# Three-stride attention and the second expert sorting in one unrolled stage, on one NeuronCore

## The chip, the cores and the metric

The kernel runs on one core of one Trainium2 chip. What counts is the device time of one execution in microseconds; the median of the kernel before is 2400.16 us over three runs (2399.35 to 2404.34).

## The reference

An input of 256 images of 128 channels and 7 x 7 places goes through four layers: a windowed attention with a bias table, a group norm with a single-head attention, a plain attention with a mixture of experts (8 experts of hidden width 192, the best 2 for each token), and the layer that the change is in. Cut to that layer:

```python
t = t + _L3_attn_ref(_ln_t(t), Wq, bq, Wk, bk, Wv, bv)   # t: 256 images, 49 tokens, 128 channels
t = t + _L3_ffn_ref(_ln_t(t), Wr, br, W1, b1, W2, b2)

# _L3_attn_ref: x + positional encoding, then 8 heads of 16
for sc in (1, 2, 4):                       # every key, every 2nd, every 4th
    scores = einsum('bhqd,bhkd->bhqk', qh, kh[::sc]) * scale
    outs.append(einsum('bhqk,bhkd->bhqd', softmax(scores), vh[::sc]))
out = mean(outs)
# _L3_ffn_ref: the router's top 2 of 8 experts for each token, hidden 512
combine = zeros(N, E).at[arange(N), top2].add(sel_w / sum(sel_w))
out = einsum('ne,end->nd', combine, gelu(x @ W1 + b1) @ W2 + b2)
```

## The kernel before

The activations stay in SBUF as X, 128 channels by 12544 tokens in fp32, through the whole kernel. The program is a row of stages, each a block of its own in which every engine has its own instruction stream and the engines meet through semaphores only; a barrier stands between two stages. In order: `heads_phase` (windowed attention), `single_phase` (group norm and its attention), `token_dispatch_phase` (plain attention and the first sorting, `d2`), `blocks_phase` (experts, `moe2`), `combine_phase`, `scales_phase` (three-stride attention), `dispatch_phase` (the second sorting, `d3`), `blocks_phase` (`moe3`), `final_phase`.

`scales_phase` (L1156) works on 32 groups of 8 images, 392 tokens each. It runs in steps, one for each group, and each step has four quarters p = 0 to 3, one for each pair of images. `pair(s, p, ahead)` names the pair that is `ahead` pairs further than pair 4s + p. The stages of the work on a pair or a group lie at different distances, so that the engines work on different groups at once: PE computes scores 3 pairs ahead (L1307), DVE takes the maximum of each key class and subtracts it 2 pairs ahead (L1403, L1407), ACT takes the exponential 1 pair ahead (L1628), DVE sums it (L1416), POOL multiplies the probabilities 8 pairs behind (L1528), PE turns them 9 pairs behind (L1332), ACT copies them out (L1646), and PE multiplies them with the values 10 pairs behind (L1350). The weights of the three strides are worked out once for a group from the class maxima and sums, by turns on DVE (`highest`, `totals`, `factors`), POOL (`lower`, `parts`, `shares`) and ACT (`lowered`). The norm of a group (DVE, L1392) runs 2 groups ahead. The bias and scale of the output are on ACT (L1655), the residual on POOL (L1543). Four quarters of a step are written out by hand in a fixed order for each engine; `over_steps` (L720) unrolls the first and last steps and loops over four steps at a time between them.

The class `Dispatch` (L1724) sorts tokens by expert. For a chunk of 4 tiles of 128 tokens: PE turns the tiles (`turn`, L1828) and computes the router's logits (`logits`, L1839); DVE takes the statistics (`stats`, L1946, L1953); ACT makes the reciprocal root (`rstd`) and DVE the negated mean (`negmean`, L1961); ACT writes the normed rows (`norm`, L1898); DVE scales the logits (`scale`, L1970), takes the two highest (`choose`) and counts; PE adds up ranks (`positions`); ACT and DVE add the gate columns (`gate`, `names`, `weigh`), DVE the row numbers (`place`); and POOL sends each row twice, to the region of either expert, by an indirect DMA of 128 rows of 132 floats (`scatter`, L2093). There are 98 tiles, so 196 scatters. Three buffers of rows go round, and a buffer's scatters must have landed before it is written again. Beside this, ACT and DVE split the weights of the 8 experts in a high and a low part (L1876, L1937), which SP loads and stores.

`dispatch_phase` (L2389) is nothing but these steps, with four PSUM banks for the turned tiles. `token_dispatch_phase` runs the same class beside an attention, unrolled, with POOL free for the scatters alone.

## Time and profile before

| what | value |
|---|---|
| median of three runs | 2400.16 us |
| profiled execution | 2404.97 us |
| its span | 2403.2 us |
| PE busy | 1784.2 us, 74% of the span |
| DVE busy | 1668.8 us, 69% |
| POOL busy | 1428.9 us, 59% |
| ACT busy | 1370.0 us, 57% |
| mean granted clock of TensorE | 0.861 of 2.4 GHz |

The profiled execution took 1.8 us more than its span, which runs from the first to the last instruction, and 4.8 us more than the median. The busy shares are means over stages with different limits, so a stage's own stretch has to be read. Times in the rows are microseconds from the span's start; PEld is the load of PE's weights, and PEclk is the granted clock as a share of 2.4 GHz.

### The profile page before, as it was taken

The page shows a single profiled execution, that of the slowest core. Times are in us where ns is not written, and L with a number is a line of the kernel's source. Part 1 is how long each engine was busy: PE and PEld are TensorE (multiplying, and loading weights), DVE is VectorE, ACT ScalarE, POOL GpSimd, SP SyncE. Part 2 cuts the span into 40 slices and gives each one's busy share as a digit, 9 for nine tenths or more (in the row PEclk, how much of TensorE's full clock was granted, in tenths as well). Part 3 has the DMA queues.
Part 4 walks back from the last instruction along what each step waited for, and adds up shares of the span by engine and source line. Part 5 has one row for each costly group of instructions (what it writes and reads, how often), then busy time and mean ns, then how long its engine had stood idle before and what let it go on. Part 6 is the DMA issues. An engine that isn't in the chain of part 4 may idle for free. (4 is left out here: it accounts for less than half of the span.)

```text
span 2403.2 us, 53239 instructions
## 1 busy us (share of the span) xinstructions
PE 1784.2 (74%) x16241; PEld 1241.7 (52%) x16241; DVE 1668.8 (69%) x4819; ACT 1370.0 (57%) x2989; POOL 1428.9 (59%) x1509
## 2 busy tenths in 40 slices
PE   7999997997777527777647888886333159999983
PEld 3555554774555415555433555554322147777763
DVE  5888886884878626656546898884654447888864
ACT  5777774564666325555406898883322147777760
POOL 4565562110577737767763667764777737767765
PEclk9999998998988569998958999995555579999995
DMA  6000000001311146665450000002611347777747
GB/s 118 9 0 0 0 1 1 1 0 41 104 55 55 55 124 182 179 174 161 140 218 1 2 0 0 0 1 57 211 64 54 90 159 232 232 233 225 231 150 321
DMA packets 169793, 233.09 MB, mean 97 GB/s; under 512 B 60032, under 2 KB 131957, under 8 KB 162190
## 3 DMA queue, kind: packets, MB, share of 16 engines
q1 hardware_dynamic: 142446, 172.32, 24.2%
q0 software_dynamic: 26880, 52.27, 6.4%
q10 hardware_dynamic: 288, 6.42, 0.6%
q8 instruction: 75, 1.23, 0.2%
q14 instruction: 104, 0.85, 0.1%
HBM read 155.37 MB, written 79.23 MB: 98 GB/s over the span
## 5 line engine op out<-in xcount | busy, mean ns | idle before, releaser
L2689 POOL DMA_INDIRECT expert_out<-moe_yr,moe_to x448 | 495.8, 1107 | 260.1 <-DVE moe_yr L2668 137.5
L2093 POOL DMA_INDIRECT expert_rows<-d_row,d_pos x392 | 380.6, 971 | 198.9 <-issue 177.5
L2604 ACT ACTIVATE moe_ah<-moe_hps,moe_w 128x512 f32<-128x512 f32 (+1 forms) x336 | 230.1, 685 | 209.4 <-PE moe_hps L2554 207.1
L2645 DVE TENSOR_TENSOR moe_hl<-moe_ah,moe_hh 128x512 fp32r<-128x512 f32 (+1 forms) x336 | 235.5, 701 | 101.1 <-ACT moe_hh L2609 95.2
L1898 ACT ACTIVATE d_row<-d_xt,d_nm,d_drs 128x128 f32<-128x128 f32 x196 | 73.8, 456 | 181.6 <-DMA expert_rows<-d_row,d_pos 179.0
L550 POOL TENSOR_TENSOR window_pr<-window_pr,window_rc 113x392 f32<-113x392 f32 x128 | 108.9, 851 | 106.5 <-DVE window_rc L494 106.4
L2552 PE MATMUL moe_hps<-moe_xh,moe_w 128*128 128x512 f32 (+1 forms) x336 | 139.0, 414 | 37.6 <-DMA moe_w<-moe_split 28.6
L1839 PE MATMUL d_small<-d_wgc,X 128*128 128x8 f32 x392 | 74.7, 318 | 113.3 <-DVE d_at L2035 113.3
L2540 PE MATMUL moe_xps<-ident,moe_xb 128*128 128x128 f32 x448 | 73.4, 289 | 113.1 <-DMA moe_xb<-expert_rows 113.0
L2564 PE MATMUL moe_yps<-moe_hh,moe_w 128*128 128x512 f32 (+1 forms) x336 | 144.5, 430 | 0.9 <-DVE moe_hl L2645 0.9
L538 POOL TENSOR_TENSOR window_sc<-window_sc,window_mx 113x392 f32<-113x392 f32 x128 | 107.8, 842 | 50.4 <-DVE window_mx L468 49.5
L2554 PE MATMUL moe_hps<-moe_xh,moe_w 128*128 128x512 f32 (+1 forms) x336 | 134.8, 401 | 0.0
L2553 PE MATMUL moe_hps<-moe_xl,moe_w 128*128 128x512 f32 (+1 forms) x336 | 134.8, 401 | 0.0
L2565 PE MATMUL moe_yps<-moe_hl,moe_w 128*128 128x512 f32 (+1 forms) x336 | 134.0, 399 | 0.0
L2566 PE MATMUL moe_yps<-moe_hh,moe_w 128*128 128x512 f32 (+1 forms) x336 | 133.9, 398 | 0.0
L1839 PEld LDWEIGHTS d_small<-d_wgc,X 128*128 128x128 f32 x392 | 73.6, 280 | 116.2 <-DVE d_at L2035 116.2
L2540 PEld LDWEIGHTS moe_xps<-ident,moe_xb 128*128 128x128 f32 x448 | 54.2, 146 | 144.3 <-DMA moe_xb<-expert_rows 135.6
L1332 PE MATMUL scales_ptps<-ident,scales_pr 113*128 113x113 f32 x512 | 90.7, 287 | 48.7 <-DVE scales_sc L1407 33.8
L2634 DVE TENSOR_TENSOR moe_xl<-moe_xps,moe_xh 128x512 fp32r<-128x512 f32 x112 | 76.4, 682 | 66.7 <-ACT moe_xh L2597 66.7
L1528 POOL TENSOR_TENSOR scales_pr<-scales_pr,scales_fac 113x416 f32<-113x416 f32 x128 | 114.7, 898 | 12.5 <-DVE scales_fac L1447 12.5
L657 ACT ACTIVATE window_pt<-window_ptps 128x452 f32<-128x452 f32 x128 | 69.8, 545 | 90.0 <-PE window_ptps L334 89.9
L2609 ACT ACTIVATE moe_hh<-moe_ah 128x512 fp32r<-128x512 f32 (+1 forms) x168 | 106.2, 632 | 5.3
(270 smaller groups left out, 5185.2 us busy)
## 6 DMA issues: line engine op xcount, KB each, us to landing
moe_w<-moe_split SPq DMA_DIRECT2D x56, 1026.5 KB, 5.2
moe_xb<-expert_rows SPq DMA_DIRECT2D x112, 264.0 KB, 3.0
moe_w<-moe_split SPq DMA_DIRECT2D x56, 449.5 KB, 3.5
c_yy<-expert_out SPq DMA_DIRECT2D x28, 448.0 KB, 6.5
final_yy<-expert_out SPq DMA_DIRECT2D x28, 448.0 KB, 7.0
expert_out<-moe_yr,moe_to POOLq DMA_INDIRECT x448
X<-in_x SPq DMA_DIRECT2D x32, 196.0 KB
expert_rows<-d_row,d_pos POOLq DMA_INDIRECT x392, 2.3
```

What stands on the lines that cost most here:

```text
L1839: last = pe.matmul(self.small[:, i * EXPERTS:(i + 1) * EXPERTS], self.sh.X[:, (t0 + i) * C:(t0 + i + 1) * C], self.wgc[:, :], start=True, ...
L2093: pool.indirect_dma_start(out=self.rows_dram, out_offset=bass.IndirectOffsetOnAxis(ap=self.pos[j][:, i, k:k + 1], axis=0), in_=self.row[j] ...
L2540: last = pe.transpose(xps[:, t * C:(t + 1) * C], xb[b % NX][:, t, 0:C], ident[:, :])
L2552: pe.matmul(out, ww[:, W1H + k * P:W1H + (k + 1) * P], xh[j][:, :], start=True, stop=False)
L2553: pe.matmul(out, ww[:, W1H + k * P:W1H + (k + 1) * P], xl[j][:, :], start=False, stop=False)
L2554: pe.matmul(out, ww[:, W1L + k * P:W1L + (k + 1) * P], xh[j][:, :], start=False, stop=True).then_inc(h_mm, 1)
L2564: pe.matmul(out, ww[0:P, W2H + k * C:W2H + (k + 1) * C], high, start=(k == 0), stop=False)
L2565: pe.matmul(out, ww[0:P, W2H + k * C:W2H + (k + 1) * C], low, start=False, stop=False)
L2566: pe.matmul(out, ww[0:P, W2L + k * C:W2L + (k + 1) * C], high, start=False, stop=(k == K - 1)).then_inc(y_mm, 1)
L2604: act.activation(ah[n % NH][0:P, :], hps[n % 3][0:P, :], func, bias=bias(b, k)[0:P]).then_inc(h_done, 1)
L2645: dve.tensor_tensor(hl[n % NH][0:P, :], ah[n % NH][0:P, :], hh[n % NH][0:P, :].bitcast(F32), ALU.subtract).then_inc(hl_done, 1)
L2689: pool.indirect_dma_start(out=y_dram, out_offset=bass.IndirectOffsetOnAxis(ap=to[j][:, t:t + 1], axis=0), in_=yr[j][:, t, :], in_offset=No ...
```

## The change

`scales_phase` and `dispatch_phase` go, and `scales_dispatch_phase` does the work of both. The steps are fully unrolled, from s = -3 to 37. Chunks of the second sorting hold 3 tiles (384 tokens) and not 4, 32 of them and one of 2. In step s, PE, DVE and ACT sort chunk s - 4, and POOL sends the scatters of chunk s - 5, six in a row, behind its last quarter. One PSUM bank holds three turned tiles and, in its last quarter, logits and ranks; to free banks, the centred tile and the queries share one, and the variance uses the bank of the values' products. The factor 1/3 goes into the value weights at the start, so the residual, its bias included, is one DVE instruction from PSUM; ACT's output copy and POOL's addition go. Both halves of the values' copy are on ACT. `shares` and `lowered` come one place earlier. The first sorting keeps its chunks.

```diff
-CHUNKS = chunk_tiles()
+CHUNKS_D2 = chunks_of([4] * 24 + [2])
+CHUNKS_D3 = chunks_of([3] * 32 + [2])
...
+        def steps(body):
+            for s in range(-LEAD, NG + LATE + 3):
+                body(Step(s, s))
...
+            def turn_rows(c):
+                pe.wait_ge(res_done, min(c + 1, NG))
+                if c >= 1:
+                    pe.wait_ge(d.normed, c)
+                d.logits(pe, c, c)
+                d.turn(pe, c)
...
+            def ranks(c):
+                pe.wait_ge(d.normed, c + 1)
+                d.positions(pe, c, c + 1)
...
             def body(s):                                  # PE
                 for p in range(PAIRS):
                     turn(*pair(s, p, -9), pair(s, p, 3))
+                    if p == 0:
+                        turn_rows(chunk(s, -4))
                     scores(*pair(s, p, 3))
+                    if p == 3:
+                        ranks(chunk(s, -4))
...
+            def residual(at):
+                dve.wait_ge(pv_mm, (at.g + 1) * PAIRS)
+                dve.scalar_tensor_tensor(out=X[:, cols(at.g)], in0=ops_[:, 0:T], scalar=b_use[:, 2:3], in1=X[:, cols(at.g)],
+                                         op0=ALU.add, op1=ALU.add).then_inc(res_done, 1)
             def body(s):                                  # DVE
+                c = chunk(s, -4)
                 for p in range(PAIRS):
+                    if p == 2:
+                        residual(s.ahead(-3))
                     shift(*pair(s, p, 2))
+                    if p == 1 and c is not None:
+                        d.negmean(dve, c)
+                        d.scale(dve, c)
                     total(*pair(s, p, 0))
                     if p == 0:
                         norm(s.ahead(2))
+                        if c is not None:
+                            d.stats(dve, c)
+                        if due(s.g - 1) and s.g % 3 == 1 and s.g // 3 <= EXPERTS:
+                            d.split_low(dve, s.g // 3 - 1)
                     if p == 1:
                         highest(s)
+                            d.choose(dve, c)
+                    if p == 2:
+                            d.count_up(dve, c)
                     if p == 3:
                         factors(s.ahead(-1))
+                            d.weigh(dve, c)
+                            d.place(dve, c)
...
             def body(s):                                  # POOL
                     if p == 2:
                         lower(s)
-                    if p == 3:
-                        shares(s.ahead(-1))
-                        residual(s.ahead(-3))
+                    if p == 2:
+                        shares(s.ahead(-1))
+                    c = chunk(s, -5)
+                    if c is not None and p == PAIRS - 1:
+                        d.scatter(pool, c)
...
+                        act.wait_ge(d.scaled, c + 1)      # ACT, p == 1
+                        d.norm(act, c)
...
-            scales_phase(nc, sh, scales)
-        dispatch_phase(nc, sh, "d3", MOE3, w3, rows_dram)
+            scales_dispatch_phase(nc, sh, scales, "d3", MOE3, w3, rows_dram)
```

On POOL, one step of the attention before, the last that is unrolled ahead of the loop, from its first quarter on (`scales_pr` with the quarter's number are the probabilities):

```order
L1528 TENSOR_TENSOR scales_pr_0<-scales_pr_0,scales_fac 113x8x52
L1537 TENSOR_TENSOR scales_xn<-scales_xn,pos 128x8x49
L1528 TENSOR_TENSOR scales_pr_1<-scales_pr_1,scales_fac 113x8x52
L1509 TENSOR_TENSOR scales_part<-scales_ef,scales_sm 113x384
L1528 TENSOR_TENSOR scales_pr_2<-scales_pr_2,scales_fac 113x8x52
L1497 TENSOR_TENSOR scales_low<-scales_mx,scales_top 113x128
L1498 TENSOR_TENSOR scales_low<-scales_mx,scales_top 113x64
L1528 TENSOR_TENSOR scales_pr_3<-scales_pr_3,scales_fac 113x8x52
L1519 TENSOR_TENSOR scales_wf<-scales_ef,scales_rc 113x384
L1543 TENSOR_TENSOR X<-X,scales_ot 128x392
```

The same step on POOL in the changed kernel:

```order
L2014 TENSOR_TENSOR scales_pr_0<-scales_pr_0,scales_fac 113x8x52
L2023 TENSOR_TENSOR scales_xn<-scales_xn,pos 128x8x49
L2014 TENSOR_TENSOR scales_pr_1<-scales_pr_1,scales_fac 113x8x52
L1995 TENSOR_TENSOR scales_part<-scales_ef,scales_sm 113x384
L2014 TENSOR_TENSOR scales_pr_2<-scales_pr_2,scales_fac 113x8x52
L1983 TENSOR_TENSOR scales_low<-scales_mx,scales_top 113x128
L1984 TENSOR_TENSOR scales_low<-scales_mx,scales_top 113x64
L2005 TENSOR_TENSOR scales_wf<-scales_ef,scales_rc 113x384
L2014 TENSOR_TENSOR scales_pr_3<-scales_pr_3,scales_fac 113x8x52
L1563 DMA expert_rows<-d_row,d_pos 107008x132
L1563 DMA expert_rows<-d_row,d_pos 107008x132 x5
```

The residual on X is gone, the shares stand a place earlier, and six scatters stand ahead of the next step's first probabilities.

On DVE in the changed kernel, the third quarter of a step and the start of the fourth (`scales_ops` are the products with the values, `scales_tot` and `scales_rc` the totals and their reciprocals, `d_` are tiles of the sorting):

```order
L1924 SCALAR_TENSOR_TENSOR X<-scales_ops,scales_b_use,X 128x392
L1874 TENSOR_REDUCE scales_mx<-scales_sps 113x32
L1878 TENSOR_TENSOR scales_sc<-scales_sps,scales_mx 113x416
L1905 TENSOR_REDUCE scales_tot<-scales_part 113x96
L1909 RECIPROCAL scales_rc<-scales_tot 113x96
L1887 TENSOR_REDUCE scales_sm<-scales_pr_2 113x32
L1466 CAST d_idf<-d_idx 128x6
L1470 TENSOR_TENSOR d_pick<-iota,d_idf 128x48
L1476 TENSOR_TENSOR d_seen<-d_pick 128x24
L1479 TENSOR_REDUCE d_more<-d_seen 128x8
L1483 TENSOR_TENSOR d_count<-d_count,d_more 128x8
L1874 TENSOR_REDUCE scales_mx<-scales_sps 113x32
```

Before, this quarter held the shift, the sum, the totals and the copy of the values; now the residual stands ahead of the shift, the totals ahead of the sum, and the sorting's counts behind it.

## Rows read from the trace of the kernel before

**Rows 1.** Busy time by stretch: us, PE, PEld, DVE, ACT, POOL (instructions), PEclk, DMA share, GB/s

```profile
1300.00:1640.00 340.00, 293.34 (x4490) 176.37 (x4486) 299.73 (x565) 294.69 (x581) 233.02 (x295) 0.96 0.00 1
1683.00:1918.00 235.00, 70.20 (x403) 59.45 (x403) 121.67 (x815) 55.87 (x211) 179.49 (x183) 0.50 0.32 104
```

**Rows 2.** Timeline at the borders: start, us, engine, line, instruction [idle before <- releaser]

```profile
1253.00 1.99 POOL L1478 MEMSET scales_pr<- 113x96 f32 x16 [4.07 <-POOLq L101]
1325.23 0.57 DVE L1392 TENSOR_TENSOR scales_xn<-scales_cen,scales_rs 128x392 f32<-128x392 f32 x1 [0.66 <-ACT scales_rs L1599]
1928.58 0.95 POOL L2093 DMA_INDIRECT expert_rows<-d_row,d_pos  x1 [0.30 <-issue]
1939.54 1.28 ACT L2589 ACT_TABLE_LOAD   x1 [33.03 <-PEq L101]
```

**Rows 3.** Groups by line, sorting stage, 1683 to 1918: busy us, mean ns | idle before

```profile
L2093 POOL DMA_INDIRECT expert_rows<-d_row,d_pos x183 | 179.9, 983 | 55.8 <-issue 55.5 <-DVE d_row L2027 0.3
L1961 DVE SCALAR_TENSOR_TENSOR d_nm<-d_mv,d_drs 128x4 f32<-128x4 f32 (+1 forms) x23 | 3.7, 162 | 51.5 <-ACT d_drs L1888 51.5
```

**Rows 4.** Timeline of DVE, one step of the attention, 1449.5 to 1462

```profile
1449.95 0.57 DVE L1392 TENSOR_TENSOR scales_xn<-scales_cen,scales_rs 128x392 f32<-128x392 f32 x1 [1.26 <-ACT scales_rs L1599]
...
1452.96 0.59 DVE L1403 TENSOR_REDUCE scales_mx<-scales_sps 113x32 f32<-113x416 f32 x1 [0.20 <-PE scales_sps L1307]
...
1456.05 0.69 DVE L1456 COPY scales_vbd<-scales_vps 52x512 f32<-52x512 f32 x1
...
1461.39 0.57 DVE L1392 TENSOR_TENSOR scales_xn<-scales_cen,scales_rs 128x392 f32<-128x392 f32 x1 [0.67 <-ACT scales_rs L1599]
```

**Rows 5.** Groups by line of POOL, attention, 1300 to 1640

```profile
L1528 POOL TENSOR_TENSOR scales_pr<-scales_pr,scales_fac 113x416 f32<-113x416 f32 x120 | 107.8, 899 | 12.5 <-DVE scales_fac L1447 12.5
L1509 POOL TENSOR_TENSOR scales_part<-scales_ef,scales_sm 113x384 f32<-113x384 f32 x30 | 30.1, 1004 | 38.9 <-ACT scales_ef L1637 38.9
L1537 POOL TENSOR_TENSOR scales_xn<-scales_xn,pos 128x392 f32<-128x392 f32 x28 | 28.9, 1033 | 56.8 <-DVE scales_xn L1392 56.8
L1519 POOL TENSOR_TENSOR scales_wf<-scales_ef,scales_rc 113x384 f32<-113x384 f32 x29 | 25.2, 868 | 0.0
L1497 POOL TENSOR_TENSOR scales_low<-scales_mx,scales_top 113x128 f32<-113x128 f32 x30 | 12.4, 414 | 0.0
L1498 POOL TENSOR_TENSOR scales_low<-scales_mx,scales_top 113x64 f32<-113x64 f32 x30 | 9.2, 306 | 0.0
```

**Rows 6.** The scatters of the first sorting stage, 600 to 960

```profile
L2093 POOL DMA_INDIRECT expert_rows<-d_row,d_pos x196: 954/958/1142, 618.6 to 865.3; - x196
```

**Rows 7.** One line of the convolution stage, its bias and residual: ns min/median/max

```profile
L1045 DVE SCALAR_TENSOR_TENSOR X<-conv_ops,conv_b_use,X x32: 615/620/627, 419.8 to 558.8; 128x392 f32 x24, 128x392 f32<-128x392 f32 x8
```

**Rows 8.** Timeline of DVE, one chunk of the sorting stage

```profile
1702.32 0.19 DVE L1970 TENSOR_TENSOR d_lg<-d_small,d_drs 128x32 f32<-128x32 f32 x1 [1.44 <-PE d_small L1839]
...
1706.37 1.19 DVE L1937 TENSOR_TENSOR d_wl<-d_raw,d_wh 128x1024 f32<-128x1024 f32 x1
1707.48 0.16 DVE L1961 SCALAR_TENSOR_TENSOR d_nm<-d_mv,d_drs 128x4 f32<-128x4 f32 x1
...
1708.63 0.17 DVE L2045 CAST d_pos<-d_spot 128x8 uint32<-128x8 f32 x1
```

**Rows 9.** Timeline, the start of the second sorting stage

```profile
1682.63 1.19 DVE L1937 TENSOR_TENSOR d_wl<-d_raw,d_wh 128x1024 f32<-128x1024 f32 x1
1682.74 1.91 POOL L2093 DMA_INDIRECT expert_rows<-d_row,d_pos  x1 [0.30 <-issue]
```

**Rows 10.** Busy time by stretch, the first sorting stage

```profile
650.00:700.00 50.00, 38.07 (x331) 28.94 (x330) 42.23 (x232) 33.98 (x115) 37.80 (x41) 0.93 0.17 55
750.00:800.00 50.00, 37.39 (x286) 30.05 (x286) 36.90 (x209) 28.13 (x94) 37.81 (x41) 0.78 0.17 55
```

**Rows 11.** Timeline of PE, attention, high clock and low

```profile
1452.33 0.56 PE L1307 MATMUL scales_sps<-scales_kbd,scales_qt 64*64 64x196 f32 x8
1623.02 0.93 PE L1307 MATMUL scales_sps<-scales_kbd,scales_qt 64*64 64x196 f32 x8
```

More of the change, by code:

```diff
@@ L1153, in _, with __init__, tiles_of @@
             over_steps(act, body, LEAD)
-def scales_phase(nc, sh, weights):
+class Experts:
+    def __init__(self, hidden):
+        self.hidden = hidden
+        self.part = C if hidden % C == 0 else 96
+        self.chunks = hidden // self.part
+        self.half = hidden + self.chunks * C
+        self.bias_at = 2 * self.half
+        self.width = 2 * self.half + self.chunks + 1
+MOE2, MOE3 = Experts(192), Experts(512)
+def tiles_of(c):
+    return range(c * CHUNK, min(TILES, (c + 1) * CHUNK))
@@ L1162, in scales_phase, with sorting_steps, scales_dispatch_phase @@
+def sorting_steps(quads, groups_done):
+    turns, step = [], 0
+    for c, t0, nt, o in quads:
+        while groups_done(step) * T < (t0 + nt) * C:
+            step += 1
+        turns.append(step)
+        step += 1
+    return turns
+def scales_dispatch_phase(nc, sh, weights, kind, e, wsplit, rows_dram):
     SCALES = 3
@@ L1219, in scales_phase, with chunk, _ @@
         block = ctx.enter_context(nc.Block())
+        def steps(body):
+            for s in range(-LEAD, NG + LATE + 3):
+                body(Step(s, s))
+        def chunk(s, ahead):
+            c = s.g + ahead
+            return c if 0 <= c < len(d.chunks) else None
+        @block.sync
+        def _(sp):
+            d.weights(sp)
+            d.pads(sp)
         def pair(s, p, ahead):
@@ L1368, in body @@
                         var(s.ahead(3))
-            over_steps(pe, body, LEAD, LATE)
+            steps(body)
+            d.totals(pe)
         @block.vector
@@ L1662, in v_out @@
                     act.wait_ge(pv_mm, (at.g - 1) * PAIRS)
-                dst, src = v_places(at, 0)
-                act.activation(dst, src, ACT.Copy).then_inc(v_left, 1)
+                for r in range(2):
+                    dst, src = v_places(at, r)
+                    last = act.activation(dst, src, ACT.Copy)
+                last.then_inc(v_done, 1)
             def body(s):
+                c = chunk(s, -4)
                 for p in range(PAIRS):
@@ L2101, in sorting_steps @@
-def sorting_steps(groups_done):
-    turns, step = [], 0
-    for c, t0, nt, o in QUADS:
-        while groups_done(step) * T < (t0 + nt) * C:
-            step += 1
-        turns.append(step)
-        step += 1
-    return turns
+                        if c is not None:
+                            d.names(act, c)
+                        if due(s.g) and s.g % 3 == 0 and s.g // 3 <= EXPERTS:
+                            d.split_high(act, s.g // 3 - 1)
+            steps(body)
 def token_dispatch_phase(nc, sh, kind, e, wsplit, rows_dram):
@@ L2160, in chunks @@
         def chunks(step):
-            return [c for c, q in enumerate(LAST_QUAD) if turns[q] == step]
+            return [c for c, q in enumerate(d.last_quad) if turns[q] == step]
         @block.sync
@@ L2232, in _ @@
                 for c in chunks(s - 2):
[L2233 removed]
+                    d.positions(pe, c, len([k for k in range(len(d.chunks)) if turns[d.last_quad[k]] <= s - 1]))
                 if group(s):
@@ L2244, in _ @@
                 for c in chunks(s):
-                    d.logits(pe, c, len([k for k in range(len(CHUNKS)) if turns[LAST_QUAD[k]] <= s - 2]))
+                    d.logits(pe, c, len([k for k in range(len(d.chunks)) if turns[d.last_quad[k]] <= s - 2]))
             d.totals(pe)
@@ L2462, in _ @@
+            for c in range(len(d.chunks)):
                 d.scatter(pool, c)
```

853 lines of the change are left out of this document (388 added, 465 removed).

## The prediction

> **What bounds the kernel now.** I first read the busy time by stretch. In the attention of the three strides, 340 us of its steady part, DVE is busy 299.7 us, ACT 294.7, PE 293.3 and POOL only 233.0; in the sorting stage behind it POOL is busy 179.5 of 235 us, and PE 70.2 and DVE 121.7 [rows 1]. The reader is to see two neighbouring stages with opposite limits. The borders of the stages come from the timeline: the attention starts at 1253.00, the last scatter at 1928.58, and the first work of the expert stage behind it at 1939.54 [rows 2]. The two stages together take 1939.54 - 1253.00 = 686.5 us.
>
> The groups by line say what sets the second stage: 183 scatters take 983 ns each and POOL is idle 0.30 us before each for "issue", with hardly another releaser [rows 3]. So POOL sends one scatter in (179.9 + 55.8) / 183 = 1.29 us, and 196 of them make the stage; everything else there waits. In the attention one group of images takes 11.44 us: two norms of the centred tile start at 1449.95 and 1461.39, and between them DVE stands still only 0.20 us, before a maximum, and 0.67 us, before the second norm [rows 4]. DVE sets this stage, with ACT close behind.
>
> **What the change does, by step.** The scatters go to POOL in the attention's own steps, six in each, and the sorting work of 3 tiles goes to DVE, ACT and PE there. The stage of its own (with its starting loads, and its first chunk before a scatter can go) is gone. I work out the length of a step X and then count steps.
>
> *POOL.* Four probability products at 899 ns, 1.00 for the parts, 1.03 for the position, 0.87 for the shares, 0.41 + 0.31 for the two differences; the residual leaves POOL [rows 5]: 3.60 + 3.62 = 7.22 us. Six scatters at the undisturbed spacing, 0.958 + 0.30 us as in the first sorting stage [rows 6], are 7.55. POOL needs 14.8 us.
>
> *DVE.* From 11.44 the copy of the values goes (0.69, now on ACT) [rows 4]; the residual comes, with the bias in one instruction that reads PSUM, as in the convolution stage: 0.62 [rows 7]. The sorting of 4 tiles took 4.05 us from the scaled logits to the end of the statistics, and 1.23 from the negated mean to the next scatter's release (1707.48 to 1708.71, 0.08 behind the start of the last row) [rows 8]: 5.3. With 3 tiles, one of four maxima, index searches, statistics and aggregations goes, about 0.6 in all: 4.7. Eight subtractions that split the weights, 1.19 each [rows 8], spread over 27 steps are 0.33. Sum: 11.44 - 0.69 + 0.62 + 4.7 + 0.33 = 16.4 us. The 0.87 us of idle time in 11.44 stays in it. I keep it because the longer step gives more slack to the old waits, but DVE gets two new ones: for PE's transposes of the three tiles, which now stand between a turn and the next scores, and for ACT's reciprocal root before the negated mean. Bounds: no waiting at all puts X at 16.4 - 0.87 = 15.5; the 51.5 / 23 = 2.2 us that DVE stands a chunk before the negated mean in the sorting stage [rows 3], on top of the 0.87, put it at 18.6. I take the present 0.87 alone, since it is from the stage with the longer work to wait behind.
>
> *ACT and PE.* ACT is busy 294.7 / 30 = 9.8 us a step; it loses the scaled output (0.57), gains the other half of the values and about 2 us of sorting: 12. PE is busy 293.3 / 30 = 9.8 and gains three transposes, six small products and the ranks, about 1.4 at the high clock: 11.2. Both stay under 16.4.
>
> *The burst.* The new wait is on POOL's queue: behind the six scatters stand the next step's probabilities, for which PE's turn and, behind it, the scores in program order wait. After DVE's reciprocal POOL has 0.87 + 0.90 + 7.55 + 0.90 = 10.2 us until the first pair of the next step is ready; turn and scores add 1.1, so the scores stand at 11.3. DVE begins the shift that reads them 16.4 - 1.3 (totals) - 1.1 (the shift) = 14.0 us after its reciprocal. The burst is hidden, by 2.7 us. If that cover went, each us of it would be added to X.
>
> *Shared interface.* One scatter took 1.91 us where DVE ran the weights' subtraction, which reads two SBUF tiles, beside it; undisturbed ones take 0.958 [rows 6, 9]. Eight of them cost POOL 8 x 0.95 = 7.6 us, 0.3 per step, and POOL has 1.6 to spare: nothing on the path. The Trainium skill (GPSIMD Engine Reference, Key points) says that POOL shares its SBUF interfaces with DVE and contends with DVE instructions that have two SBUF inputs. By that rule the small products of the sorting would stretch scatters too. The first sorting stage speaks against it: all 196 scatters beside the same small DVE work and an attention lay between 954 and 1142 ns [rows 6]. The sum stays at zero here.
>
> *The count.* The steps up to the norm of group 6, at 1325.23, have no sorting in them [rows 2]; the start is about 2 us later, since DVE and PE now wait for the sorting's constants. From there 27 steps of X carry both. After the norm's place in step 31 POOL still needs 18.4 us to the end of that step's burst (9.0 on DVE to the reciprocal, then 0.87 + 0.90 + 7.55), then 13.0 (3.60 + 1.00 + 0.87 + 7.55) and 11.2 (3.60 + 7.55) for the two steps that still have probabilities, three times 7.6 and a last 5.1: 52.1; the sorting's own chain, by the spacing of its steps some 8 us a chunk, runs beside it. Landing and barrier are 10.0, as from 1929.53 to 1939.54 now [rows 2]. The expert stage then starts at 1325.2 + 2 + 27 x 16.4 + 18.4 + 52.1 + 10.0 = 1407.7 + 27 x 16.4 = 1850.5, which is 89.0 us earlier than 1939.5. What is behind it does not change. The profiled execution took 2404.97 us, so 2316.0; it lies 4.8 above the median of the three runs, 2400.16, and against that I predict **2311 us**.
>
> **Rivals.**
> 1. *DVE without its waits, POOL at its floor.* X = 15.1 from POOL's 14.8 and the 0.3 of stretched scatters, and 0.1 for the handover, 15.2; the stage ends at 1818, 2279 us. For it: the first sorting stage runs exactly at its scatters. Against: DVE alone has 15.5 without a wait.
> 2. *PE's clock is low for part of the time.* At the busy share of the first sorting stage (38.1 and 37.4 of 50 us) the granted clock was 0.93 and 0.78, so between 1.2 and 2.4 GHz by turns [rows 10]. PE would be busy only 11.2 of 16.4 us here. Scores for a pair take 0.56 us at the high clock and 0.93 at the low one [rows 11], 1.66 times as long: PE then needs 11.2 x 1.66 = 18.6 us and, with its present 1.6 of waiting, X = 20.2. With three tenths of the time low, as those two rows have it on average, X = 1 / (0.7 / 16.4 + 0.3 / 20.2) = 17.4: 1877.5, 2338 us. Against: the slack of 5 us takes short dips.
> 3. *PE's clock stays low throughout: slower than before.* X = 20.2 gives 1407.7 + 545.4 = 1953.1, 13.6 us later than now, 2414 us. It decides from X = 19.7 on, where the stage ends as before. For it: the second sorting stage had 0.50 throughout [rows 1]. Against: at the low clock PE would be busy 18.6 of 20.2 us, and at 293 of 340 the attention's clock was 0.96 [rows 1].
>  The Trainium skill (TensorE: Matmul & The Clock Gate, HAM oscillation) says that gaps in PE's work make the gate fall back to half rate. By that rule a step with a long wait behind the burst would fall back each time, which is this rival; without such a wait rival 2 at most.
> 4. *The burst is not hidden.* If the 7.55 us came on top of the present step, X = 19.0 and 2381 us. It needs turn, scores and shift to be waiting at once, which the 2.7 us above speak against.
>
> **How the numbers follow.** Forecast 0.45, rival 1 0.17, rival 2 0.22, rival 4 0.06, rival 3 and other ways beyond X = 19.7 0.08, the strip around no change 0.02. About 0.2% (4.8 us) is what a measurement of this kernel can tell from no change. The range runs from below rival 1, where the tail is also a little shorter, 2270, to X = 18.6, 1909.9, 2370. Faster 0.90, same 0.02, slower 0.08.
>
> **What would show it.** The spacing of the attention's norms in steady state near 16.4; POOL busy about 13.3 of it with its "issue" gaps; DVE busy about 14.5; scatters near 0.96 us, none above 1.2 but those beside the weights' subtraction; the wait of PE's turn for POOL's probabilities small; DVE's waits for PE before the statistics and for ACT before the negated mean, together near 1 us a step; the granted clock at 0.85 or more; some 50 us of scatters behind the last group. I am wrong if the spacing is beyond 18.6, if PE's turns wait for POOL by more than 1 us each step, or if the clock stays at 0.5.

## The result and the profile after

The changed kernel takes 2389.26 us (median of five runs, 2388.34 to 2391.54) beside 2402.08 us of the kernel before on the same chip: a ratio of 0.995, 95% interval 0.9935 to 0.9964. It is faster by 12.8 us, which is clear of the noise but only 0.5%, where 89 us were forecast, and it lies outside the range. The profiled span went from 2403.2 to 2389.8 us.

The page's busy times of the changed kernel, and its two sorting and attention lines:

```profile
PE 1850.0 (77%) x16257; PEld 1271.8 (53%) x16257; DVE 1759.3 (74%) x4940; ACT 1380.3 (58%) x3028; POOL 1400.3 (59%) x1477
...
L1563 POOL DMA_INDIRECT expert_rows<-d_row,d_pos x392 | 377.7, 964 | 180.0 <-issue 175.4
...
L2014 POOL TENSOR_TENSOR scales_pr<-scales_pr,scales_fac 113x416 f32<-113x416 f32 x128 | 115.6, 905 | 6.6 <-DVE scales_fac L1918 6.0
```

DVE is busy 90.5 us longer than before, for work that hardly changed. The merged stage begins at 1253.86 and the expert stage's first instruction comes at 1926.85, so it takes 673.0 us; the two stages before took 686.5. The steady part, busy time by stretch, and the norms of groups 6, 8 and 31 on DVE's timeline (`scales_xn`), the last two 23 steps apart:

```profile
1360.00:1800.00 440.00, 331.98 (x3785) 203.86 (x3783) 391.03 (x1124) 285.95 (x648) 293.70 (x342) 0.77 0.14 46
```

```profile
1326.88 0.57 DVE L1863 TENSOR_TENSOR scales_xn<-scales_cen,scales_rs 128x392 f32<-128x392 f32 x1 [1.40 <-ACT scales_rs L2082]
...
1361.07 0.57 DVE L1863 TENSOR_TENSOR scales_xn<-scales_cen,scales_rs 128x392 f32<-128x392 f32 x1 [1.06 <-ACT scales_rs L2082]
...
1805.49 0.57 DVE L1863 TENSOR_TENSOR scales_xn<-scales_cen,scales_rs 128x392 f32<-128x392 f32 x1 [0.99 <-ACT scales_rs L2082]
```

A step is (1805.49 - 1361.07) / 23 = 19.3 us and not 16.4, and DVE is busy 391 of 440 us in it (columns as in [rows 1]), 89%. Where its time went stands in the groups by line of the same stretch, DVE alone; the last row is one that is not held up:

```profile
L1426 DVE SCALAR_TENSOR_TENSOR d_nm<-d_mv,d_drs 128x3 f32<-128x3 f32 x23 | 45.3, 1969 | 3.9 <-ACT d_drs L1353 3.5
L1402 DVE TENSOR_TENSOR d_wl<-d_raw,d_wh 128x1024 f32<-128x1024 f32 x7 | 25.6, 3663 | 0.1
L1476 DVE TENSOR_TENSOR d_seen<-d_pick 128x24 bf16<-128x24 f32 x23 | 18.3, 794 | 0.8
L1470 DVE TENSOR_TENSOR d_pick<-iota,d_idf 128x48 f32<-128x48 f32 x23 | 10.8, 471 | 0.8
L1454 DVE TENSOR_TENSOR d_gap<-d_top 128x3 f32<-128x3 f32 x23 | 7.1, 308 | 0.8
L1897 DVE TENSOR_TENSOR scales_top<-scales_mx 113x32 f32<-113x32 f32 x23 | 4.6, 201 | 0.0
```

The first five of them as the kernel before has them in its sorting stage, with 4 tiles instead of 3:

```profile
L1937 DVE TENSOR_TENSOR d_wl<-d_raw,d_wh 128x1024 f32<-128x1024 f32 x6 | 7.3, 1209 | 7.3 <-ACT d_wh L1876 7.3
...
L2000 DVE TENSOR_TENSOR d_pick<-iota,d_idf 128x64 f32<-128x64 f32 (+1 forms) x22 | 4.9, 223 | 0.8
L2006 DVE TENSOR_TENSOR d_seen<-d_pick 128x32 bf16<-128x32 f32 (+1 forms) x22 | 4.7, 213 | 0.8
...
L1989 DVE TENSOR_TENSOR d_gap<-d_top 128x4 f32<-128x4 f32 (+1 forms) x22 | 3.6, 165 | 0.8
L1961 DVE SCALAR_TENSOR_TENSOR d_nm<-d_mv,d_drs 128x4 f32<-128x4 f32 (+1 forms) x22 | 3.6, 162 | 51.5 <-ACT d_drs L1888 51.5
```

A negated mean of 3 numbers a partition takes 1969 ns instead of 162. All five have two inputs in SBUF (two tensors, or for `d_seen` and `d_gap` two parts of one); so has the sixth, at a place where POOL stands still. Per step that is 1.81 + 0.58 + 0.25 + 0.14, and 7 x 2.45 / 23 = 0.75 for the splits: 3.5 us. What POOL does meanwhile is seen when the two timelines of one step are laid side by side, POOL's first:

```profile
1468.03 0.87 POOL L2005 TENSOR_TENSOR scales_wf<-scales_ef,scales_rc 113x384 f32<-113x384 f32 x1 [3.41 <-DVE scales_rc L1909]
1468.86 0.90 POOL L2014 TENSOR_TENSOR scales_pr<-scales_pr,scales_fac 113x416 f32<-113x416 f32 x1
1469.90 1.01 POOL L1563 DMA_INDIRECT expert_rows<-d_row,d_pos  x1 [0.15 <-issue]
...
1476.27 0.96 POOL L1563 DMA_INDIRECT expert_rows<-d_row,d_pos  x1 [0.30 <-issue]
1477.25 0.91 POOL L2014 TENSOR_TENSOR scales_pr<-scales_pr,scales_fac 113x416 f32<-113x416 f32 x1
1478.11 1.03 POOL L2023 TENSOR_TENSOR scales_xn<-scales_xn,pos 128x392 f32<-128x392 f32 x1
1479.09 0.90 POOL L2014 TENSOR_TENSOR scales_pr<-scales_pr,scales_fac 113x416 f32<-113x416 f32 x1
1479.95 0.99 POOL L1995 TENSOR_TENSOR scales_part<-scales_ef,scales_sm 113x384 f32<-113x384 f32 x1
1480.90 0.88 POOL L2014 TENSOR_TENSOR scales_pr<-scales_pr,scales_fac 113x416 f32<-113x416 f32 x1
...
1486.88 0.87 POOL L2005 TENSOR_TENSOR scales_wf<-scales_ef,scales_rc 113x384 f32<-113x384 f32 x1 [3.41 <-DVE scales_rc L1909]
```

```profile
1478.68 0.59 DVE L1878 TENSOR_TENSOR scales_sc<-scales_sps,scales_mx 113x416 f32<-113x416 f32 x1
1479.20 2.60 DVE L1426 SCALAR_TENSOR_TENSOR d_nm<-d_mv,d_drs 128x3 f32<-128x3 f32 x1
1481.73 0.17 DVE L1435 TENSOR_TENSOR d_lg<-scales_sorted,d_drs 128x24 f32<-128x24 f32 x1
...
1486.05 0.75 DVE L1909 RECIPROCAL scales_rc<-scales_tot 113x96 f32<-113x96 f32 x1
```

POOL's row of five elementwise products behind the six scatters ends at 1481.78. The negated mean, begun at 1479.20, ends at 1481.80. **A loop** goes through both engines: from DVE's reciprocal POOL waits for no other engine, through shares, product, burst and row, from 1468.03 to 1481.78, 13.75 us; only then does DVE get past the negated mean, and needs 5.1 us to the next reciprocal; POOL goes on at 1486.88. 13.75 + 5.10 = 18.85 us is this step. It is not the only one: of the 18 negated means between 1360 and 1700, 15 end within 0.05 us behind the row's last product, and the other three stand behind a split of 4.9 or 5.6 us that had waited for the row in their place. The waits say the same without naming it: POOL stands 3.41 us for the reciprocal in every one of the 23 steps, though in the step above DVE works without a gap meanwhile.

### The profile page after: what moved, and what is told of

The parts are those of the page before. It is cut to its first block and busy times, and to the rows that moved or that the text cites. A ratio compares the mean times of both kernels' runs of the same rounds, so it can differ in the third digit from the quotient of the medians.

```text
span 2389.8 us, 52820 instructions
## 1 busy us (share of the span) xinstructions
PE 1850.0 (77%) x16257; PEld 1271.8 (53%) x16257; DVE 1759.3 (74%) x4940; ACT 1380.3 (58%) x3028; POOL 1400.3 (59%) x1477
## 5 line engine op out<-in xcount | busy, mean ns | idle before, releaser
L1780 PE MATMUL scales_ptps<-ident,scales_pr 113*128 113x113 f32 x512 | 113.9, 332 | 135.4 <-DVE scales_sc L1878 122.5
L1780 PEld LDWEIGHTS scales_ptps<-ident,scales_pr 113*128 113x128 f32 x512 | 74.0, 173 | 189.1 <-DVE scales_sc L1878 113.8
L2129 ACT ACTIVATE scales_pt<-scales_ptps 128x452 f32<-128x452 f32 x128 | 69.7, 545 | 125.0 <-PE scales_ptps L1780 124.6
L2632 DVE CAST moe_hh<-moe_ah 128x512 fp32r<-128x512 f32 (+1 forms) x168 | 88.3, 525 | 27.1 <-ACT moe_ah L2593 27.1
```

Of the source, the lines that this page charges most:

```text
L1780: last = pe.transpose(ptps[:, hp * R:(hp + 1) * R], pr[at.r][p][:, 2 * hp:2 * hp + 2, :].rearrange("q h k -> q (h k)"), ident[0:R, 0:R])
```

## The experiments

X is the spacing of the norms of groups 8 to 31. The stage runs from POOL's first fill to the expert stage's table load; its start moves by some us between kernels, since the stages ahead of it do. PE's granted clock is that of 1400 to 1700. Every kernel ran beside the kernel before (medians 2399.6 to 2402.8). The expectations say VectorE for DVE, GpSimd for POOL, ScalarE for ACT and TensorE for PE.

| kernel | median us | ratio to before (95%) | stage us | X us | PE clock |
|---|---|---|---|---|---|
| changed kernel | 2389.3 | 0.995 (0.9935 to 0.9964) | 673.0 | 19.3 | 0.77 |
| negated mean later | 2381.4 | 0.991 (0.988 to 0.994) | 669.5 | 19.25 | 0.76 |
| negated mean, one input | 2377.5 | 0.990 (0.987 to 0.994) | 661.6 | 18.9 | 0.76 |
| all moved | 2367.9 | 0.987 (0.983 to 0.991) | 654.8 | 18.6 | 0.79 |
| three pairs of scatters | 2324.6 | 0.968 (0.9645 to 0.972) | 610.7 | 16.9 | 0.81 |
| two scatters early | 2336.1 | 0.973 (0.971 to 0.976) | 621.1 | 17.4 | 0.82 |
| unlocked | 2312.1 | 0.963 (0.960 to 0.967) | 588.1 | 16.1 | 0.86 |
| unlocked, three pairs | 2342.3 | 0.975 (0.972 to 0.979) | 614.7 | 17.1 | 0.80 |
| unlocked, one put back | 2363.8 | 0.985 (0.983 to 0.987) | 634.1 | 17.8 | 0.81 |
| unlocked, statistics later | 2457.9 | 1.023 (1.020 to 1.026) | 729.5 | 21.4 | 0.72 |
| unlocked, PE busier | 2317.6 | 0.9655 (0.964 to 0.967) | 587.2 | 15.9 | 0.94 |
| unlocked, two early | 2317.3 | 0.966 (0.964 to 0.968) | 589.8 | 16.2 | 0.84 |

### Is it the two inputs, and does the time go when they are moved?

My first theory (A) took the held-up instructions as a price per instruction. Three kernels remove that price in different ways.

```diff
-                    if p == 1 and c is not None:
-                        d.negmean(dve, c)
-                        d.scale(dve, c)
...
                         highest(s)
                         if c is not None:
+                            d.negmean(dve, c)
+                            d.scale(dve, c)
                             d.choose(dve, c)
```

> The negated mean (128x3, two SBUF inputs) and the scaled logits go behind the first and second maximum of the same quarter, to a place where GpSimd has come to the end of its row of products. In the changed kernel the negated mean took 1.94 us on average, 0.16 in the kernel before. Theory A (a VectorE instruction with two SBUF inputs can't start while GpSimd runs elementwise products one behind the other): it takes 0.2 to 0.5 us, the step goes from 19.3 to about 17.7 us, 27 x 1.7 = 46 us less, 2343 us. Rival B (the 1.94 us are the wait for ScalarE's reciprocal root, put down to the instruction): the time moves with it into another place of VectorE, 2389 within 5 us. Rival C (TensorE at its low clock sets the step, VectorE's length fills slack): the instruction gets short but VectorE's idle time grows by as much, over 2380 us.

```diff
-        dve.scalar_tensor_tensor(out=self.nm[q % 2][:, 0:nt], in0=self.mv[q % 2][:, 0:nt, 0], scalar=-1.0, in1=self.rs[c % 2][:, o:o + nt], ...)
+        for i in range(nt):
+            last = dve.tensor_scalar(self.nm[q % 2][:, i:i + 1], self.mv[q % 2][:, i, 0:1], self.rs[c % 2][:, o + i:o + i + 1], -1.0,
+                                     ALU.mult, ALU.mult)
```

> The negated mean stays at its place, behind the same wait, but is written as three instructions that each read one SBUF tensor (a column of the means) and take the reciprocal root as a per-partition scalar. Theory A (two SBUF inputs are what is held up): each takes 0.06 to 0.2 us, together under 0.5, the step loses 1.5 us, 27 x 1.5 = 41 us less, 2348 us. Rival B (wait for ScalarE's root): the first of the three takes about 1.8 us, 2389. Rival C (TensorE sets the step): the three are short and the time stays over 2380 us. A fourth outcome, that the scalar operand is held up like a second tensor, would show as three long instructions or one long one, and a time of 2389 or more.

The third moves `negmean` and `scale` as the first, `count_up` behind the shift of quarter 3, and `split_low` behind `place`:

> All three stretched pieces on VectorE are moved to where GpSimd runs no elementwise product: the negated mean behind the maxima, the counting (comparison 0.47, sum over both choices 0.79 us) behind the shift of the last quarter and the eight subtractions that split the weights (3.87 us each on average, 1.19 in the kernel before) to the end of the step, both beside the scatters. Theory A: these take 0.2, 0.22, 0.21 and 1.2 us again; per step 1.78 + 0.25 + 0.58 = 2.6 us go, and 8 x 2.7 = 21 us for the splits: 27 x 2.6 + 21 = 91 us, 2298 us, if nothing else becomes the bound; the step is then 15.9 us. Rival C (TensorE at its partly low clock comes next): the step stops at 17 to 17.5, 2330 to 2345 us. Rival B: over 2380. The scatter beside a split should take 1.9 us and lengthen nothing.

All three missed the time: 2381, 2377 and 2368 us where 2343, 2348 and 2298 stood. But each moved instruction became short, as the theory said. Groups by line of DVE, 1400 to 1740, of the kernel with the negated mean later, with one input, and with all moved:

```profile
L1897 DVE TENSOR_TENSOR scales_top<-scales_mx 113x32 f32<-113x32 f32 x17 | 29.5, 1733 | 0.0
L1402 DVE TENSOR_TENSOR d_wl<-d_raw,d_wh 128x1024 f32<-128x1024 f32 x6 | 28.2, 4700 | 0.1
...
L1426 DVE SCALAR_TENSOR_TENSOR d_nm<-d_mv,d_drs 128x3 f32<-128x3 f32 x17 | 2.5, 148 | 0.0
```

```profile
L1899 DVE TENSOR_TENSOR scales_top<-scales_mx 113x32 f32<-113x32 f32 x18 | 22.3, 1238 | 0.0
...
L1427 DVE TENSOR_SCALAR d_nm<-d_mv,d_drs 128x1 f32<-128x1 f32 x54 | 8.1, 206 | 3.1 <-ACT d_drs L1353 2.6
```

```profile
L1897 DVE TENSOR_TENSOR scales_top<-scales_mx 113x32 f32<-113x32 f32 x18 | 56.9, 3159 | 0.0
L1402 DVE TENSOR_TENSOR d_wl<-d_raw,d_wh 128x1024 f32<-128x1024 f32 x6 | 7.4, 1238 | 0.0
...
L1426 DVE SCALAR_TENSOR_TENSOR d_nm<-d_mv,d_drs 128x3 f32<-128x3 f32 x19 | 2.8, 146 | 0.0
```

The negated mean is at 148 ns behind the maxima, or at three times 206 with one SBUF tensor behind the same wait for ACT: rival B, that the 1.9 us were ACT's reciprocal root, falls. The hold-up went to the next instruction with two SBUF inputs, the second maximum `scales_top`, which took 0.20 us before and now takes 1.24 to 3.16 us. So a step does not pay per instruction; whichever comes first waits for POOL, and the loop stays. With everything else moved, the loop alone is 18.6 us.

### Cutting the loop on POOL's side

```diff
-                    if c is not None and p == PAIRS - 1:
-                        d.scatter(pool, c)
+                    if c is not None and 1 <= p <= d.chunks[c][1]:
+                        d.scatter(pool, c, [p - 1])
```

> The six scatters go out two at a time, behind the first three products of probabilities of the next stretch of the step, in place of all six at its end. GpSimd's products then don't stand in one row of 4.5 us behind the burst. Theory A: the negated mean waits for the rest of one product only, 0.2 to 1.0 us in place of 1.94, and the step loses about 1 us: 2360 us; VectorE's maxima may be stretched to 0.5 us as in the kernel before. Rival B (ScalarE's root): 1.94 stays and so does 2389. Rival D (the burst's place is what keeps the step short, by the slack behind it): TensorE's turns wait longer for the products and the time rises over 2395 us.

2324.6 us: the gain is 65 us where theory A had 29. The negated mean took 0.25 us on average. The size of the gain told me that the burst stood in the loop, and the second theory (A2, the loop as laid out above) came from it. It is tested with the smaller edit: one tile's two scatters go out ahead of `shares`, the other four stay.

```diff
+                    c = chunk(s, -5)
                     if p == 2:
                         lower(s)
+                        if c is not None:
+                            d.scatter(pool, c, [0])
                     if p == 2:
                         shares(s.ahead(-1))
...
-                        d.scatter(pool, c)
+                        d.scatter(pool, c, range(1, d.chunks[c][1]))
```

> Two of the six scatters go out one stretch earlier, between the two differences and the shares, where GpSimd waits 3.4 us a step for VectorE's reciprocal; four stay at the step's end. Nothing else is changed, and all instructions of VectorE stay at their places. Theory A2 (a loop: from VectorE's reciprocal GpSimd runs the shares, one product, the burst and a row of five products without a gap, 13.8 us, and VectorE's first instruction with two SBUF inputs behind the burst waits for the row's end; from there VectorE needs 5.1 us to the next reciprocal; together the 18.9 us of the step): the loop gets 2 x 1.26 = 2.5 us shorter, the step 16.8 us or VectorE's own 16.4, the negated mean is back under 1 us, 2389 - 27 x 2.5 = 2322 us. Rival A1 (the row of products must be broken up by scatters, as in the run with three pairs): the negated mean stays near 1.9 us and the time over 2375 us. Rival C (TensorE's partly low clock sets the step): over 2375.

2336.1 us where 2322 stood, X 17.4: 1.9 of the 2.5 us came, the negated mean took 0.46 us on average, and nothing on DVE was touched. A1 (the row must be broken up) had over 2375 and falls. That 0.6 is missing fits what is left: `count_up` still stands beside the shares and the product, with 0.79 us for the sum.

### Cutting it on DVE's side, and closing it again

```diff
-                dve.tensor_tensor(top2[:, :], m[:, :, 0], m[:, :, 2], ALU.max).then_inc(top2_done, 1)
+                dve.tensor_reduce(top2[:, :], m[:, :, 0:CLASSES:2], AX_X, ALU.max).then_inc(top2_done, 1)
...
+            last = dve.scalar_tensor_tensor(out=self.lg[:, i, :], in0=self.small[:, i * EXPERTS:(i + 1) * EXPERTS],
+                                            scalar=self.rs[c % 2][:, i:i + 1], in1=self.bg[:, :], op0=ALU.mult, op1=ALU.add)
...
-        dve.tensor_tensor(self.gap[:, 0:nt], top[:, 0:nt, 1], top[:, 0:nt, 0], ALU.subtract).then_inc(self.gap_done, 1)
+            last = act.activation(self.ex[:, i:i + 1], self.top[:, i, 0:1], ACT.Exp, bias=self.top[:, i, 1:2], scale=-1.0)
```

with the one-input negated mean, and `count_up` and `split_low` moved as above. The edits of the class `Dispatch` act in the first sorting too.

> The burst stays whole, but no VectorE instruction with two SBUF inputs is left between two bursts: the second maximum is a reduction over the two columns, the negated mean takes the reciprocal root as a per-partition scalar (three instructions), scale and bias of the logits are one instruction per tile with PSUM and the bias as inputs, the difference of the two best logits is taken by ScalarE inside its exponential, and the counting and the splits stand beside the burst. Theory A2: VectorE waits for GpSimd's row of products no longer, the loop is cut, and the step goes to VectorE's own work, about 16 us (14.5 busy and 1.3 of waits), 2389 - 27 x 3.3 = 2300 us; the second maximum takes 0.2 us. If the small instructions were held up as well though they read one tensor, the step stays at 18.6 to 19.3 and the time over 2365. Rival C (TensorE's clock): over 2340.

2312.1 us where 2300 stood, X 16.1. Busy time by stretch, and DVE's and POOL's waits, of this kernel:

```profile
1400.00:1700.00 300.00, 247.35 (x3139) 157.03 (x3131) 261.74 (x964) 237.24 (x565) 236.78 (x281) 0.86 0.18 58
```

```profile
POOL scales_wf L2006 <- DVE scales_rc L1911: 34.4, 20, 3.2
...
DVE d_dst L1413 <- PE scales_sorted L1293: 17.7, 19, 1.5
```

DVE is busy 87% of 16.1, 14.0 us a step; POOL's wait for the reciprocal is halved (34.4 / 20 = 1.7 us). Part of what is missing to 2300 lies outside the merged stage: from the first to the last scatter of the first sorting this kernel takes 258.4 us, the changed kernel 249.4. Of the six kernels with these edits of the class, five lie between 258 and 263 us there and one at 251; the others lie between 247 and 250. From this kernel one instruction is put back, the second maximum as it was:

> The kernel without held-up instructions, with one instruction put back: the second maximum (113x32) is again the larger of two SBUF columns, in place of a reduction over them; both take 0.2 us when nothing holds them. It stands on VectorE while GpSimd runs its row of products. Theory A2: this one instruction waits for the row's end, 1.5 to 3 us a step, and closes the loop again: the step goes from 16.1 to about 18.6 us (what the kernel with everything but this moved had), 2312 + 27 x 2.4 = 2377 us; at least 2350. Any theory in which the gain came from the number or the length of the small instructions, or from TensorE: 2312 within 8 us.

2363.8 us, 52 more, for one instruction of 0.2 us a step. Groups by line of this kernel, then POOL and DVE in one of its steps:

```profile
L1899 DVE TENSOR_TENSOR scales_top<-scales_mx 113x32 f32<-113x32 f32 x17 | 37.6, 2213 | 0.0
```

```profile
1428.10 0.99 POOL L1996 TENSOR_TENSOR scales_part<-scales_ef,scales_sm 113x384 f32<-113x384 f32 x1
1429.06 0.89 POOL L2015 TENSOR_TENSOR scales_pr<-scales_pr,scales_fac 113x416 f32<-113x416 f32 x1
```

```profile
1426.65 3.37 DVE L1899 TENSOR_TENSOR scales_top<-scales_mx 113x32 f32<-113x32 f32 x1
1429.94 0.27 DVE L1900 TENSOR_REDUCE scales_top<-scales_mx 113x32 f32<-113x128 f32 x1
```

It ends with POOL's last product (1429.95), 3.37 us after its start. This is the cleanest pair of the study: the same result, the same place, the same 0.2 us of work, one SBUF input or two. Its step is 17.8 us and that of the kernel with all moved 18.6, and the loop gives both. Here POOL's shares in one step of the one and of the other, with the wait ahead of them:

```profile
1433.94 0.87 POOL L2006 TENSOR_TENSOR scales_wf<-scales_ef,scales_rc 113x384 f32<-113x384 f32 x1 [2.97 <-DVE scales_rc L1911]
```

```profile
1441.62 0.87 POOL L2003 TENSOR_TENSOR scales_wf<-scales_ef,scales_rc 113x384 f32<-113x384 f32 x1 [3.70 <-DVE scales_rc L1909]
```

Between 1400 and 1720 POOL needs 13.8 us from its shares to the row's end in both. From there to the next shares it is 4.0 us with one instruction put back (3.99 to 4.02) and 4.7 with all moved (4.72 to 4.84), where the negated mean, the logits' scale and bias and their difference still stand in between: 17.8 and 18.5. With nothing held up the same distance varies from 1.25 to 3.87 us: there the loop is open.

### Both sides together

> The same edits on VectorE, and the six scatters two at a time behind the first three products. Theory A2: both remedies cut the same loop, so they don't add: the step goes from the 16.9 us of the spread scatters alone to VectorE's own 15.8, 2325 - 27 x 1.1 = 2295 us. If something else than the held-up instructions made the spread kernel's 16.9, it stays at 2320 to 2330.

A miss: 2342.3 us, slower than either remedy alone. Its groups by line and waits:

```profile
L1493 DVE TENSOR_SCALAR d_den<-d_ex 128x3 f32<-128x3 f32 x18 | 16.7, 929 | 0.0
```

```profile
DVE d_dst L1413 <- PE scales_sorted L1293: 27.4, 19, 1.7
...
PEld scales_ptps L1782 <- POOL scales_pr L2015: 22.5, 19, 1.3
```

PE's turns now wait for POOL's product, 1.2 us a step, and DVE for the turned tiles behind them, 1.4; and one instruction with a single SBUF input, which in the burst had taken 158 ns, takes 929 beside a product (671 with three pairs alone). Which of these holds the step at 17.1 was not tested. The other combination leaves the order of the products alone:

> Both remedies that keep the order of the products: no VectorE instruction that GpSimd's products can hold up, and two of the six scatters one stretch earlier, where GpSimd waits 0.9 to 1.7 us a step. Theory A2: the loop was cut by the first remedy alone, so the second adds nothing but may fill GpSimd's wait and lengthen its queue: 2305 to 2318 us, step 16.0. If the burst still set part of the 16.1 us step in another way (TensorE's turns waiting behind it), the step drops toward 15 and the time under 2300. If the earlier scatters make the shares late, over 2320.

2317.3 us, X 16.2: as A2 has it, the loop was already cut, and the second remedy gains nothing.

### TensorE's clock, and DVE's waits for TensorE

`warm` adds products whose results are overwritten, ahead of PE's waits in `turn`:

```diff
+                pe.matmul(ptps[:, 0:64], sh.centre_w[:, :], sh.centre_w[:, 0:64], start=True, stop=True, skip_group_check=True)
                 pe.wait_ge(prob_done, n + 1)
                 for hp in range(HP):
                     if hp == HP - 1:
+                        for _ in range(2):
+                            pe.matmul(ptps[:, hp * R:hp * R + 64], sh.centre_w[:, :], sh.centre_w[:, 0:64], ...)
                         scores_ready(*then)
```

> The same kernel with twelve more products of 128 by 64 a step on TensorE, whose results are overwritten, one before each wait for probabilities and two before each wait for the scores' buffer: TensorE is busier by 2 to 3 us of 16. It tells what TensorE's clock (granted 0.86 here, 0.77 in the changed kernel) is worth: if the low stretches cost (rival C), the clock goes to 0.95 or more and the step loses more than the added work, under 2300 us; if VectorE's chain sets the step and TensorE has slack, 2312 within 8 us; if TensorE has no slack, over 2325.

```profile
1400.00:1700.00 300.00, 266.12 (x3554) 194.72 (x3555) 263.77 (x968) 239.31 (x568) 238.79 (x283) 0.94 0.19 62
```

The granted clock goes from 0.86 to 0.94 in this stretch and the stage from 588.1 to 587.2 us; the whole kernel takes 2317.6 us, within the 8 us that were named. At X 16 the low stretches cost next to nothing; in the changed kernel, with its longer step, the clock was not raised, so there this is only carried over. The 0.77 there looks like a result of the longer step more than its cause: over the table the clock goes from 0.72 at 21.4 us to 0.86 at 16.1, though not in order in every pair.

> The same kernel with the sorting's statistics, negated mean, scaled logits and choice on VectorE, and the root, the normalised rows and the exponential on ScalarE, each one quarter of a step later. VectorE now waits 0.9 us a step for TensorE's three transposes before the statistics. If those waits lie on VectorE's chain, which sets the step, they go: 16.1 to about 15.2 us, 2290 us. If the wait only moves (the transposes are late by TensorE's queue, and VectorE then waits elsewhere), 2305 to 2320; if the shorter time for the rest of the chain makes ScalarE or TensorE wait, over 2320.

The worst miss, 2457.9 us, 146 over the kernel it was made from. Its waits:

```profile
DVE scales_mx L1876 <- PE scales_sps L1757: 35.8, 15, 2.4
DVE d_den L1493 <- ACT d_ex L1374: 35.5, 15, 3.0
...
DVE d_nm L1429 <- ACT d_drs L1353: 15.1, 15, 1.0
DVE X L1926 <- PE scales_ops L1799: 12.7, 15, 1.7
```

The wait for the transposes is gone, and four others of together 6.6 us a step took its place. One of the two largest is that for ACT: its exponential now stands in its queue behind the keys and the logarithm of quarter 3, and DVE's denominator, in the same quarter, waits 2.4 us for it. I read this as slack that the old order had put between the two and that I removed; no run tests it.

### The same instruction in the kernel before

`before_top` is the kernel before with the second maximum as a reduction.

> The kernel before, with the second maximum as a reduction over two columns instead of the larger of two SBUF tensors. In its attention the two-input form took 0.46 us on average (0.20 to 0.52) beside GpSimd's products, where 0.20 is its length with nothing beside it. Theory A2: this was the same hold-up, of one product's rest instead of a row's; it goes back to 0.2 us and the 32 steps lose 0.26 us each where VectorE sets them: 8 us, 2392. If it was something else: no change.

2401.45 beside 2401.61 us, ratio 0.9997 (0.998 to 1.001): no change where 8 us stood, though the instruction went from 0.47 to 0.21 us. Over the 30 steps from 1300 to 1640 that is 7.9 us less; DVE's waits for the scores grew from 4.8 to 8.0 us there and those for POOL's parts from 4.4 to 5.6, so more than half of it turned into waits. X there is 11.30 instead of 11.33. So in this attention the wait for the rest of one product cost nothing that could be measured, and DVE's own work alone does not set its step.

## Why the prediction failed

**The start and the end were right.** The norm of group 6 stands at 1326.88, where 1325.2 + 2 was assumed. The norm of group 31 is that of step 29, and two steps of 19.3 behind it, at 1844.1, begins a tail of 70.0 us to the last scatter's end (1914.08), where 18.4 + 52.1 = 70.5 were counted. Landing and barrier took 12.8 us instead of 10.0. With X = 19.14, the mean from group 6 on, the count gives 1924.6 for the measured 1926.85.

**POOL, the burst's own wait and DVE's new waits were right.** Scatters took 966 ns on average, all but one (1.09) at most 1.02 us; the turns waited for POOL 2.2 us in 350, and their weight loads 3.1; DVE's waits for the transposes and the root came to 7.8 and 2.6 us in 18 steps, 0.6 a step, where I looked for 1. DVE's sum was right too, as a sum of its own work: the kernel in which nothing is held up runs at 16.1 us where 16.4 stood, and takes 2312 us beside a forecast of 2311. That the times agree to 1 us is luck in part: its stage is 9.4 us shorter than the 597.5 that the prediction had (1850.5 - 1253.0), but begins 6.8 us later than before, and its profiled execution does not lie 4.8 us above its median, as I had taken it. And "DVE sets this stage" was too strong: with 0.26 us less of DVE's work a step, the step before went from 11.33 to 11.30.

**The step that failed is "Shared interface ... The sum stays at zero here".** I looked at one side of it: what DVE does to POOL's scatters. The row that I took, one scatter at 1.91 us beside a split [rows 9], showed DVE first and POOL held. In the merged stage POOL no longer sends scatters only, as in both sorting stages from which I took DVE's durations [rows 8]; it multiplies, and there DVE is the one held. Durations taken beside a neighbour that issues DMAs were carried over to a place beside one that reads SBUF. The term put at zero measured 3.5 us a step; with it the sum is 19.9, and with the second maximum back at 0.20 us from 0.46 it is 19.7, for 19.3 measured. It is no price per instruction, though, as the moved instructions showed: the loop sets its size. The Trainium skill (SBUF — State Buffer, Who interferes with whom) says this: a VectorE instruction with two SBUF inputs contends with a GpSimd instruction that reads SBUF; the pair of ports that they share is an exclusive lock, and the order of issue decides which of them blocks. The trace agrees, 1969 ns for 162; I had weighed the Trainium skill's sentence in the GPSIMD Engine Reference (Key points) against the first sorting stage, where scatters alone are on POOL.

**The second error is in "The burst is hidden, by 2.7 us".** The path that I checked, products, turn, scores, shift, has that slack, and the turns hardly waited. But each us of the burst delays the row of products, and the row releases DVE. Taking 2.5 us from the burst took 1.9 from the step, so the burst did lengthen the step, by another road than rival 4's. That rival's price, 19.0 us and 2381, lies near the measured 19.3 and 2389 by luck: it adds the burst to the present 11.44 us and leaves the sorting's work on DVE out.

**The other rivals.** Rival 1 did not come; even without hold-ups the step is 16.1 us. Rivals 2 and 3: the clock was 0.77, below the 0.85 that I named, and did not stay at 0.5. Raising it by other work gained nothing in the kernel where nothing is held up; in the changed kernel itself that was not tried.

## What to carry to other kernels

When work of two stages is merged, take the durations of small vector instructions from a place where the other engine does what it will do in the new one: SBUF-reading products on GpSimd beside two-input instructions on VectorE are a wait that no semaphore shows, visible only as an instruction ten times its length. If such a wait moves to the next instruction when its victim is moved, look for the loop it closes, and cut the loop: the last instruction with two SBUF inputs written as a reduction, once all the others were rewritten or moved, or two DMAs issued earlier, were worth 50 us each, where removing a single victim was worth 8 to 12. The version that came out, every two-input instruction of the loop rewritten or beside the burst, beats both kernels: 2312 us, 0.963 (0.960 to 0.967) of the kernel before. Its rewritten small instructions are in the first sorting too, which took longer with them in five of six kernels; no run here tried them in the second sorting alone.

## What the runs showed of the hardware

- A VectorE instruction that waits for GpSimd can lose at several ends of GpSimd's instructions one behind the other. The negated mean above passed two such ends before the third, the row's last, let it in, and one split began at 1496.07 and ended at 1501.71 behind five products that ended at 1500.62; its own work is 1.19 us. It is not always so: with two scatters early, 8 of 11 negated means between 1400 and 1600 began beside the parts' product, and all 8 got in at its end, ahead of the row's last product, while the second maxima of the kernel with one put back that began there waited for the last product too. What decides was not found.
- The hold-up goes both ways. In the kernel with two scatters early a product at 1484.60 took 1.88 us instead of 0.90 beside a split that had begun 0.2 us earlier, and in the changed kernel the parts' product took 1.99 to 2.01 us beside four of the eight splits and 0.98 to 1.00 otherwise.
- Instructions with a single SBUF tensor are not all free: the denominator (`tensor_scalar`, 128x3, SBUF to SBUF) took 929 ns beside a product and 158 beside a scatter, while the same form on one column (the negated mean) stayed at 206, and reductions kept their lengths. The Trainium skill (SBUF — State Buffer, Who interferes with whom) has `tensor_scalar` among the forms that can take both port pairs; the 929 ns agree with it.
- A split beside a scatter cost little in the kernel with all moved: 1.24 us for the splits, at most 1.19 for a scatter (1.26 in the kernel with nothing held up), where the one in the kernel before had 1.91 [rows 9].
